# A hybrid layer on one Trainium2 core: spaced scatters, float32 expert stages, and a mixing stage with clamps, reciprocals and inverse deviations on ScalarE

## The reference

```python
x = x + attention(_layernorm(x))   # linear relu attention, 16 heads of 8, rmsnorm and rope on q and k
x = x + experts(_layernorm(x))     # router, top 2 of 8 experts
x = x + mixing(_layernorm(x))      # token shift, k, v, r, recurrence over time, Wo
x = x + experts(_layernorm(x))
```

```python
scores = x @ Wr.T + br;  idx = top_k(scores + biases, 2);  val = softmax(scores)[idx] / sum
h = x @ Wl1[e] + bl1[e];  a, b = h[:, :256], h[:, 256:]
y += val * (silu(a) * b @ Wl2[e] + bl2[e])
```

```python
q = max(pp, u + k);  e1 = exp(pp - q);  e2 = exp(u + k - q)
y = (e1 * aa + e2 * v) / (e1 * bb + e2)       # then times sigmoid(r), then Wo
```

## Time and profile before

| | |
|---|---|
| median of three runs | 1330.14 us (1322.95 to 1336.12) |
| the profiled execution | 1346.64 us, span 1344.8 us, mean granted TensorE clock 0.798 of full |
| attention | 0 to about 332 us |
| last scatters of attention, table, first tiles | 332 to 363 us |
| first expert stage, from the first transposition to the last result landed | 362.77 to 639.37 us; its first result scatter starts at 373.51, its last at 637.27 (2.1 us before it has landed) |
| mixing, with the last scatters | 639 to 1029 us |
| second expert stage | 1029 to 1304 us |
| weighing and storing the output | 1304 us to the end |

### The profile page before, as it was taken

One profiled execution on the slowest core, in us unless ns is written; L12 is line 12 of the kernel. 1 busy time (PEld: TensorE's weight loads), 2 busy tenths in 40 slices (PEclk: granted clock), 3 DMA queues, 4 the chain that ended last, 5 costly groups with the idle time before them and its releaser, 6 DMA issues.

```text
span 1344.8 us, 21163 instructions
## 1 busy us (share of the span) xinstructions
PE 855.2 (64%) x5110; PEld 697.5 (52%) x5111; DVE 918.4 (68%) x2976; ACT 659.9 (49%) x1788; POOL 623.3 (46%) x597
## 2 busy tenths in 40 slices
PE   3777777742178887776457667657423777887850
PEld 1665566542177887765123333323223777876750
DVE  5688888645465655555299999999953565655657
ACT  3676666611154444444576766655322444444435
POOL 3024444433545554545215555675434555555440
PEclk9788877856599888899677787787655899889885
DMA  7022222212222222221311222211092222222239
GB/s 223 16 60 79 78 79 80 65 53 68 83 75 74 68 76 69 71 58 49 110 60 63 69 83 86 94 47 38 30 254 66 71 69 75 73 70 69 62 97 315
DMA packets 144880, 111.79 MB, mean 83 GB/s; under 512 B 15779, under 2 KB 135724, under 8 KB 144464
## 3 DMA queue, kind: packets, MB, share of 16 engines
q1 hardware_dynamic: 126928, 77.58, 20.6%
q0 software_dynamic: 17920, 33.88, 7.9%
HBM read 62.84 MB, written 50.64 MB: 84 GB/s over the span
## 4 chain that ended last, share of the span: by engine, by line
DVE 31%; PE 31%; issue 13%; ACT 7%; another core or an unknown queue 5%; POOL 5%; DMA 4%; DVEq 2%; ACTq 1%; SPq 0%; POOLq 0%
PE banks L965 8%; PE banks L946 5%; POOL queue_dram L508 4%; PE banks L948 4%; PE banks L947 4%; DVE rope_c L1414 3%; PE banks L828 2%; PE banks L854 2%; DVE stats L1095 2%; PE banks L955 2%; ACT gated L690 1%; DVE gated L1239 1%; DMA out<-xmid 1%; DVE tile_up L1253 1%
## 5 line engine op out<-in xcount | busy, mean ns | idle before, releaser
L519 POOL DMA_INDIRECT result_dram<-ytile,result_row x288 | 283.9, 986 | 274.3 <-DVE ytile L1259 191.8
L508 POOL DMA_INDIRECT queue_dram<-hffn,place_i x192 | 222.9, 1161 | 205.8 <-DVE place_i L1177 120.6
L946 PE MATMUL banks<-xt_parts,tile_up 128*128 128x256 f32 x584 | 185.8, 318 | 87.4 <-DVE tile_up L1253 81.6
L1239 DVE SCALAR_TENSOR_TENSOR gated<-banks,tile_bias,gated 128x256 f32<-128x256 f32 x292 | 127.8, 479 | 99.9 <-ACT gated L690 76.4
L965 PE MATMUL banks<-wdown_sb,gated 128*128 x1152 | 171.2, 297 | 20.6 <-DVE gated L1239 20.5
L947 PE MATMUL banks<-xt_parts,tile_up 128*128 128x256 f32 x584 | 172.9, 296 | 0.0
L948 PE MATMUL banks<-xt_parts,tile_up 128*128 128x256 f32 x584 | 172.7, 296 | 0.0
L946 PEld LDWEIGHTS banks<-xt_parts,tile_up 128*128 128x128 f32 x584 | 119.9, 205 | 100.7 <-DVE xt_parts L1248 61.9
L965 PEld LDWEIGHTS banks<-wdown_sb,gated 128*128 128x128 f32 x1152 | 157.8, 211 | 24.3 <-issue 24.2
L690 ACT ACTIVATE gated<-banks,tile_bias 128x256 f32<-128x256 f32 x292 | 121.9, 470 | 97.4 <-PE banks L948 70.2
L696 ACT ACTIVATE xt_parts<-banks 128x256 fp32r<-128x256 f32 x150 | 57.8, 386 | 215.2 <-PE banks L955 171.7
(11 more groups left out here) (210 smaller groups left out, 1986.8 us busy)
## 6 DMA issues: line engine op xcount, KB each, us to landing
xtiles<-queue_dram SPq DMA_DIRECT2D x160, 130.0 KB
qkv<-result_dram SPq DMA_DIRECT2D x24, 512.0 KB, 4.3
x_dram<-xres SPq DMA_DIRECT2D x32, 256.0 KB
result_dram<-ytile,result_row POOLq DMA_INDIRECT x288
xin<-x SPq DMA_DIRECT2D x16, 256.0 KB
xold<-x SPq DMA_DIRECT2D x16, 256.0 KB
expo<-w_up SPq DMA_DIRECT2D x2, 2048.0 KB, 9.3
xin<-x_dram SPq DMA_DIRECT2D x16, 256.0 KB
```

Source lines behind the costliest of these rows:

```text
L508: nc.gpsimd.indirect_dma_start(queue_dram, bass.IndirectOffsetOnAxis(ap=place_i[s][:, at:at + 1], axis=0), hffn[s][c][:, j, :], None).then ...
L519: nc.gpsimd.indirect_dma_start(result_dram, bass.IndirectOffsetOnAxis(ap=result_row[i][:, h:h + 1], axis=0), ytile[i][:, h, :], None, boun ...
L946: nc.tensor.matmul(ps_up[at][:, h, :], hi, xt_parts[at][:, 0, :], start=True, stop=False)
L1239: last = nc.vector.scalar_tensor_tensor(gated[at][:, h, :], ps_up[at][:, HCH + h, :], tile_bias[(i + 1) % STEP][:, HCH + h:HCH + h + 1], g ...
```

## The change

**On POOL**, after every one of the 256 scatters of `scatter` and the 288 of `experts`, `space()` writes the tile `spacer` (128x16), waits for its own write and clears the semaphore. `pace` is gone, and so is the cast of the weights at the start.

**In the expert stages** the splitting is gone. PE makes each output block of `up` from one float32 product; ACT copies the transposed tile out of PSUM once (`empty_x`); the tile's `up` weights (256 KB) come from DRAM by a DMA that ACT issues, into four slots, four tiles ahead; DVE no longer splits, copies weights or subtracts tables. The loops now take 12 tiles a round, with six slots for tiles and results and three for `gated`; `up` runs two tiles ahead and transpositions four. The last round stands by itself, and no tile past the 72nd is loaded. The 2 MB load of the raw weights ahead of each stage is gone.

**In mixing** the two clamps of the past exponents move from DVE to ACT (as ReLU with a sign, and the exponential with scale -1). The reciprocals of the denominator move to ACT, as an inverse square root and a square per half (`invert`), and DVE only multiplies (`divided`). `exponents` now stands behind `divided`, ahead of the wait for `xres`. The deviations of both normalisations in mixing are taken by ACT as an inverse square root (`inverse_deviations`), and the DVE reciprocals of them are gone. Attention keeps its way.

```diff
-STEP = 8
+STEP = 12
+SLOTS = 6
+ROUNDS = XTILES // STEP
+WSLOTS = 4
+GSLOTS = 3
+SPACER = 16
...
-def pace(m, pair):
-
-    if pair == 1:
-        pool.wait_ge(attn_turned[1], m + 1)
...
-def scatter(m, s, paced):
+def space():
+
+    nc.gpsimd.memset(spacer[:], 0.0).then_inc(spaced, 1)
+    pool.wait_ge(spaced, 1)
+    pool.sem_clear(spaced)
+
+def scatter(m, s):
 
     pool.wait_ge(place_ready, m)
     pool.sem_inc(place_taken, 1)
     for c in range(HALVES):
         for j in range(TPC):
-            if paced and c + j:
-                pace(m, c * TPC + j)
-                pool.sem_inc(place_taken, 1)
             for k in range(TOPK):
                 at = (c * TPC + j) * TOPK + k
                 nc.gpsimd.indirect_dma_start(
                     queue_dram, bass.IndirectOffsetOnAxis(ap=place_i[s][:, at:at + 1], axis=0),
                     hffn[s][c][:, j, :], None).then_inc(queued[s][c], 16)
+                space()
 
...
-pool.wait_ge(experts_in, 16 * len(EXPERTS))
-nc.gpsimd.tensor_copy(up_hi[:], up_raw).then_inc(hi_ready, 1)
-with pool.Fori(0, 2) as n:
-    scatter(n * 2 + 1, 1, True)
-    scatter(n * 2 + 2, 0, True)
-scatter(5, 1, True)
-scatter(6, 0, False)
-scatter(7, 1, False)
-scatter(8, 0, False)
+with pool.Fori(0, BATCH // 2) as n:
+    scatter(n * 2 + 1, 1)
+    scatter(n * 2 + 2, 0)
...
+
+def inverse_deviations(c, m, var, moment, rstd, ready):
+
+    act.wait_ge(var[c], m)
+    nc.scalar.activation(rstd[c][:], moment[c][:, :, 1], ACT.Abs_reciprocal_sqrt, bias=ln_eps[:, 0:1]).then_inc(ready[c], 1)
 
...
-        act.wait_ge(up_ready, t + (2 + f * N_UP))
-        at = (i + 1) % 2
+        act.wait_ge(bias_ready, done(f, t))
+        act.wait_ge(up_ready, done(f, t))
...
-    def split_x(t, i):
-
-        act.wait_ge(xtile_turned, t + (4 + f * N_TURN))
-        nc.scalar.activation(xt_parts[(i + 3) % 2][:, 0, :], ps_xt[(i + 3) % 2], ACT.Copy).then_inc(xhi_ready, 1)
-
-    def weights(t, i, e):
-
-        nc.scalar.activation(tile_up[i % 2][:, 0, :], up_hi[:, bass.ds(e * (2 * HID), 2 * HID)].bitcast(F32), ACT.Copy).then_inc(whi_ready, 1)
+    def empty_x(t, i):
+
+        act.wait_ge(xtile_turned, done(f, t))
+        nc.scalar.activation(xt[i % 2][:], ps_xt[i % 2], ACT.Copy).then_inc(xt_ready, 1)
+
+    def weights(i, e):
+
+        nc.scalar.dma_start(tile_up[i % WSLOTS][:], w_up[:, bass.ds(e * (2 * HID), 2 * HID)]).then_inc(tile_up_in[i % WSLOTS], 16)
+
+                silu_up(first + i + 2, i + 2)
+            if i + 2 + WSLOTS < left:
+                weights(i + 2 + WSLOTS, e[i])
+            if i + 4 < left:
+                empty_x(first + i + 4, i + 4)
...
     act.wait_ge(past_expo, m)
-    nc.scalar.activation(expo[:, 2:4, :], expo[:, 2:4, :], ACT.Exp).then_inc(past_ex, 1)
+    nc.scalar.activation(expo[:, 2, :], gap_past, ACT.Relu, scale=-1.0)
+    nc.scalar.activation(expo[:, 3, :], gap_past, ACT.Relu).then_inc(clamped, 1)
+    act.wait_ge(clamped, 2 * m - 1)
+    nc.scalar.activation(expo[:, 2:4, :], expo[:, 2:4, :], ACT.Exp, scale=-1.0).then_inc(past_ex, 1)
     act.wait_ge(now_expo, m)
     nc.scalar.activation(expo[:, 0, :], gap, ACT.Relu)
-    nc.scalar.activation(expo[:, 1, :], gap, ACT.Relu, scale=-1.0).then_inc(gap_ready, 1)
-    act.wait_ge(gap_ready, m)
+    nc.scalar.activation(expo[:, 1, :], gap, ACT.Relu, scale=-1.0).then_inc(clamped, 1)
+    act.wait_ge(clamped, 2 * m)
     nc.scalar.activation(expo[:, 0:2, :], expo[:, 0:2, :], ACT.Exp, scale=-1.0).then_inc(now_ex, 1)
     act.wait_ge(r_ready, m)
     nc.scalar.activation(e_r, ps_r, ACT.Exp, scale=-1.0).then_inc(er_ready, 1)
+
+def invert(row):
+
+    act.wait_ge(den_ready, row)
+    for c in range(HALVES):
+        part = y_den[:, c * CHUNK:(c + 1) * CHUNK]
+        nc.scalar.activation(part, part, ACT.Abs_reciprocal_sqrt).then_inc(root_ready, 1)
+    for c in range(HALVES):
+        part = y_den[:, c * CHUNK:(c + 1) * CHUNK]
+        act.wait_ge(root_ready, row * HALVES + (c + 1 - HALVES))
+        nc.scalar.activation(part, part, ACT.Square).then_inc(inverted, 1)
 
...
+    invert(m - BATCH)
...
+    def up(n, i):
+
+        t = n * STEP + i
+        pe.wait_ge(xt_ready, done(f, t))
+        pe.wait_ge(tile_up_in[i % WSLOTS], loaded(f, n, WSLOTS, i))
+        if not (isinstance(t, int) and t < 2):
+            pe.wait_ge(gated_ready, done(f, t - 2) + GATED_FIRST)
         for h in range(2 * HCH):
-            cols = slice(h * P, (h + 1) * P)
-            hi, lo = (tile_up[at][:, part, cols] for part in range(2))
-            nc.tensor.matmul(ps_up[at][:, h, :], hi, xt_parts[at][:, 0, :], start=True, stop=False)
-            nc.tensor.matmul(ps_up[at][:, h, :], hi, xt_parts[at][:, 1, :], start=False, stop=False)
-            last = nc.tensor.matmul(ps_up[at][:, h, :], lo, xt_parts[at][:, 0, :], start=False, stop=True)
+            last = nc.tensor.matmul(ps_up[i % 2][:, h, :], tile_up[i % WSLOTS][:, h * P:(h + 1) * P], xt[i % 2][:],
+                                    start=True, stop=True)
         last.then_inc(up_ready, 1)
 
...
-    def down(t, i, e):
-
-        pe.wait_ge(gated_ready, t + (1 + f * N_GATE))
+    def down(n, i, e):
+
+        t = n * STEP + i
+        pe.wait_ge(gated_ready, done(f, t) + GATED_FIRST)
+        pe.wait_ge(ytile_ready, done(f, t - 2) + YTILE_FIRST)
...
+    def steps(n, left):
+
+        e = read(mybir.EngineType.PE, tile_expert[0:1, bass.ds(n * STEP, STEP)], NE - 1)
+        for i in range(STEP):
+            if i + 2 < left:
+                up(n, i + 2)
+            if i + 4 < left:
+                turn_x(n, i + 4)
+            down(n, i, e[i])
+
...
     for c in both:
         dve.wait_ge(dev_ready[c], m)
-        inverted.append(mark(nc.vector.reciprocal(rstd[c][:], dev[c][:])))
-    for c in both:
-        need(inverted[c])
         nc.vector.scalar_tensor_tensor(shift[c][:], moment[c][:, :, 0], -1.0, rstd[c][:], ALU.mult, ALU.mult).then_inc(ready[c], 1)
...
-    if f == FIRST:
-        dve.wait_ge(hi_ready, 1)
-    else:
-        dve.wait_ge(experts_in, 16 * (len(EXPERTS) + 1))
-    nc.vector.tensor_tensor(up_lo[:], up_raw, up_hi[:].bitcast(F32), ALU.subtract).then_inc(lo_ready, 1)
-
...
     need(scanned)
-    settle(nc.vector.scalar_tensor_tensor(gap_past, top[:, before], w_sb[:, 0:1], ps_k, ALU.add, ALU.subtract))
-    nc.vector.tensor_scalar(expo[:, 2, :], gap_past, 0.0, None, ALU.min)
-    nc.vector.tensor_scalar(expo[:, 3, :], gap_past, -1.0, 0.0, ALU.mult, ALU.min).then_inc(past_expo, 1)
+    nc.vector.scalar_tensor_tensor(gap_past, top[:, before], w_sb[:, 0:1], ps_k, ALU.add, ALU.subtract).then_inc(past_expo, 1)
     nc.vector.scalar_tensor_tensor(gap, ps_k, ch_sb[:, V_FIRST:V_FIRST + 1], top[:, before],
                                    ALU.add, ALU.subtract).then_inc(now_expo, 1)
...
     dve.wait_ge(er_ready, row)
-    settle(nc.vector.scalar_tensor_tensor(y_den, e_r, 1.0, y_den, ALU.add, ALU.mult))
+    nc.vector.scalar_tensor_tensor(y_den, e_r, 1.0, y_den, ALU.add, ALU.mult).then_inc(den_ready, 1)
+
+def divided(row):
+
     for c in both:
         part = slice(c * CHUNK, (c + 1) * CHUNK)
-        settle(nc.vector.reciprocal(y_den[:, part], y_den[:, part]))
+        dve.wait_ge(inverted, row * HALVES + (c + 1 - HALVES))
         nc.vector.tensor_tensor(rwkv[:, part], y_num[:, part], y_den[:, part], ALU.mult).then_inc(rwkv_ready[c], 1)
...
     outputs(m - BATCH, *scans)
     if ahead:
         scanned = maxima(m - (BATCH - 1))
+    divided(m - BATCH)
+    if ahead:
+        exponents(m - (BATCH - 1), scanned)
     for c in both:
         dve.wait_ge(xres_ready[c], m)
     moments(xres, stats2, moment2, var2_ready)
     scales_for_experts(m)
-    if ahead:
-        exponents(m - (BATCH - 1), scanned)
```

More of the change, by code:

```diff
@@ L321, in program @@
         FIRST, SECOND = 0, 1
-        N_TURN, N_WEIGHTS, N_UP, N_GATE, N_BACK = (XTILES + ahead for ahead in (3, 2, 1, 1, 0))
         PLACE_STEPS = 3
@@ new lines, in experts @@
+                act.wait_ge(table_ready, f + 1)
+                e = read(mybir.EngineType.Activation, tile_expert[0:1, 0:2 + WSLOTS], NE - 1)
+                for t in range(WSLOTS):
+                    weights(t, e[t])
+                empty_x(0, 0)
+                empty_x(1, 1)
+                for t in range(2):
+                    silu_up(t, t)
+                    weights(t + WSLOTS, e[t + WSLOTS])
+                    empty_x(t + 2, t + 2)
+                with act.Fori(0, LAST) as n:
+                    steps(n, 2 * STEP)
@@ L720, in weigh @@
+                steps(LAST, STEP)
             def weigh(y, g, done, first=0, step=1):
@@ new lines, in steps @@
+                def steps(n, left):
+                    e = read(mybir.EngineType.DVE, tile_expert[0:1, bass.ds(n * STEP, min(STEP + 4, left))], NE - 1)
+                    for i in range(STEP):
+                        if i + 2 < left:
+                            gate(n, i + 2)
+                        add_bias(n, i, e[i])
+                        if i + 3 < left:
```

(14 more changed lines are left out.)

228 lines of the change are left out of this document (88 added, 140 removed).

## The result

The changed kernel takes **1498.28 us** (median of 4 runs, 1496.29 to 1499.47), the kernel before on the same chip 1333.13 (4 runs, 1322.95 to 1338.26): ratio **1.125** (95% interval 1.118 to 1.132), 165 us slower. 1412 was forecast, with 1262 to 1450 as the range. The direction was right, the size half of what came.

The account below looks back on a forecast made before the run. POOL, with a spacer after each scatter, was to bound the expert stages and the mixing loop: 27 + 51 + 9 - 5 = +82 us, against the median of 1330.1 a forecast of 1412 us, range 1262 to 1450.

Parts of the forecast that it names:

- The spacer's mechanism: After every scatter: waiting for POOL's own write exposes the next scatter's preparation, 0.58 us per queue scatter, 0.64 per result scatter.
- part 1: Expert stages: POOL becomes the bound at 3.84 us a tile, 289 us a stage, +27 us for both.
- 0.80 us for both gaps: Expert stages: each of a tile's two result scatters starts 0.80 us after the spacer, from 0.88 less 0.08.
- Part 2: Mixing: the POOL loop of scatters, sums and statistics sets rows of 47.8 us, together +51 us.
- s: Time the spacer adds per scatter: 0.58 us for queue scatters, 0.64 us for result scatters.
- no scatter of 5 us: Sign of being right: no scatter would take 5 us any more.
- Parts 3 to 5: Last scatters of both routings +9 us, start -5 us, attention 0.
- part 3: Last scatters of both routings, where POOL alone is the path: +8.8 - 4.2 each, +9 us.
- its start: Start of attention: the L1295 pair no longer meets POOL's weight cast and the DMA queue is lighter, -5 us.
- The conversion to the median: Whole kernel: profiled execution stood 16 us above the median of 1330.1, so 1412 us was forecast, not 1429.
- Attention: 0: Attention: no pacing, 30 us of scatters still fit in 33 us a row, so no cost.
- The first rival: All scatters: preparation stays hidden behind the spacer's wait, s = 0.2 us, -59 us, 1271 us; chance 17%.

Follow-up runs that it names:

- e7: Changed kernel with space() reduced to an already met wait and the clearing of the semaphore, no write; 1423.76 us.
- e8: Changed kernel with space() reordered: wait for the previous spacer's write, clear, then write with no wait behind it; 1439.36 us.
- e1: Changed kernel without space() behind any scatter, all else kept; 1404.84 us, ratio 1.038 to the kernel before.
- e6: Changed kernel with space() cut to the clearing of the semaphore, no write and no wait; 1415.55 us.
- e10: Changed kernel with the old mixing stage, unspaced there, and the spacer behind every second scatter in attention and expert stages; 1290.66 us, ratio 0.967.
- e13: Changed kernel with old mixing unspaced, spacer behind every second scatter in attention and every fourth result scatter in expert stages; 1246.95 us, ratio 0.934.

## Why the prediction was right about the direction and wrong about the size

- **The spacer's mechanism held.** POOL is the bound in the expert stages and closes the loop in mixing, a met wait is free, and an unmet one costs 0.8 to 1.0 us (e7 and e8 against the changed kernel). For the queue's scatters 0.58 us was forecast and 0.63 measured (1.89 against 1.26).
- **The term that failed most is part 1, the result scatters: 3.84 us a tile forecast, 4.10 measured.** Taking 0.80 us for both gaps failed twice. Of the 0.08 us that were taken off for a signal from another engine most is not there (0.86 before a tile's first scatter where 0.80 was taken, 0.80 before a queue scatter where 0.74 was), and the second scatter, which the earlier trace rows never shows behind a wait, needs 1.02; the write takes 0.14, not 0.11. In each stage seven to nine tiles of 4.4 to 4.5 us and one of 6.6 come on top. From the first result scatter to the end of the last the sum gives 143 x 1.92 + 0.98 = 275.5 us, +24 for both stages (the other 3 of its +27 lie ahead of the first scatter), and they were +71: **47 of the 70 us** between the forecast +82 and the measured +151.7.
- **Part 2, mixing: +51 forecast, +74.6 measured** (72.7, and 1.9 ahead of row 9, where -1 was forecast). Per row 51.2 against 47.8: 2.2 us are scatters that run long (busy 21.8 against 19.56 us a row), 0.8 are s, and 0.7 are the gap ahead of the first sum (1.0 where 0.3 was taken); 0.3 came back elsewhere. The long scatter had a precedent in the earlier trace rows; the prediction had used it for the table subtraction alone. It had "no scatter of 5 us" among its signs of being right; rows 9 to 14 have one each.
- **Parts 3 to 5.** The last scatters of a routing with the way to the first result were to cost +6.4 each (4.6 in part 3 and 1.8 in part 1) and cost +9.0 (6.0 and 3.0; the scatters are 0.63 us longer, and the first tiles wait for two float32 blocks). Attention was to be 5 us shorter by its start and is 11.6 (row 8 begins at 320.9 instead of 332.5), but not by its start: row 1's first scatter starts at 91.5 us instead of 90.6. From row 6 to row 8 it takes 62.4 us instead of 74.8, and there the kernel before has its longest late signal, 7.9 us.
- **The conversion to the median failed.** 16 us were taken off because the profiled execution of before stood above its runs. The changed kernel's stands on its median (1498.31 against 1498.28), so the last 16 us of the 86 are this.
- **"Attention: 0" came out near by luck.** The cover (30 us of scatters in a row of 33) was not what mattered: with faster scatters attention gets slower. Row 8 begins at 386.6 us in e1, with 79 us of late signals in attention.
- **The first rival, 1271 us if the preparation stays hidden, is false.** e6, e7 and e8 hide the preparation, e8 with the write in it, and take 1416, 1424 and 1439 us. It costed the rest of the change as if PE's results reached ACT and DVE at once. What hid the gain was the late signals, 117 us of waits in the kernel before and 238 in e1, that no step of the prediction had looked at.

## What to carry to other kernels

A wait is cheap where it is met, and an unmet one ahead of an indirect DMA cost 0.80 to 1.02 us here: cost it by the first instruction after a real wait, for each instruction in the group, and not by one value. Look through the list of waits for releasers that no program line explains, and ask what else ran at that time; here they told both why scatters must be spaced and why spacing each one was too much. Give each stage its own spacing: every second scatter in attention, every fourth in the expert stages and none in mixing, with the old mixing stage, took 1247 us, where every one took 1498.

## What the runs showed of the hardware

- Results of PE reached ACT or DVE up to 12.3 us late while POOL issued indirect DMAs 0.3 us apart (e1, `out_squares`, sixteen in a row). With a gap of 0.8 to 1.0 us behind each one, or behind each second, none was late. In the mixing rows of the kernel before, of e10 and of e13, sixteen in a row held none. What in the chip holds them, and which, stays open.
- An indirect DMA that took 0.96 us took 4.3 to 5.6 us in the new mixing stage beside four DVE operations on float32 in SBUF that join without a break, and ended 0.8 us after the break; beside the same four in the old one it took 0.96 to 2.0. The Trainium skill (SBUF — State Buffer, SBUF: two separate sides) names two kinds of DVE operation that can hold up GpSimd, those in a two-port mode and those with two inputs in SBUF, the latter only against a GpSimd instruction that reads SBUF. The rows here are float32 `TENSOR_TENSOR` operations with two inputs in SBUF; no run shows that this is what holds the scatter, and it does not say why the old stage has none.
- The median of the kernel before differs between sets of runs (1333 to 1350 us); the two kernels that a fully spaced POOL bounds took 1498.28 and 1498.06 us in two of them.
